# The third layer merged into the second one's block and worked batch by batch, in a kernel of four transformer layers

## What is computed

```python
# L2 xattn: a fixed mask of crucial places, maxima and means over the channels, a convolution, two maps
crucial_features = crucial_channels * x
subcrucial_features = subcrucial_channels * x
c_max = jnp.max(crucial_features, axis=1, keepdims=True)
c_avg = jnp.mean(crucial_features, axis=1, keepdims=True) * (C / k)
...
A_S1 = _norm_active(_conv1d(crucial_x, conv_w), bn_gamma, bn_beta)
A_S2 = _norm_active(_conv1d(subcrucial_x, conv_w), bn_gamma, bn_beta)
return crucial_features * A_S1 + subcrucial_features * A_S2
```

## Time and profile before

| | us |
|---|---|
| median of 3 runs | 1889.36 |
| the runs, lowest and highest | 1887.64, 1889.57 |
| the profiled execution | 1889.23 |
| its span in the trace | 1887.5 |
| TensorE (matmul) busy | 1808.7, 96% |
| DVE busy | 1348.4, 71% |
| ScalarE busy | 636.3, 34% |
| GpSimd busy | 614.9, 33% |

### The profile page before, as it was taken

How to read it: one execution, slowest core, us unless ns; L and a number is a source line. 1 busy time by engine, 2 the same in 40 slices (tenths; PEclk the granted TensorE clock), 3 DMA queues, 4 the chain that set the end, 5 groups by cost and what they waited for, 6 DMA issues and landing times. The chain is left out here.

```text
span 1887.5 us, 29022 instructions
## 1 busy us (share of the span) xinstructions
PE 1808.7 (96%) x10418; PEld 1529.3 (81%) x10418; DVE 1348.4 (71%) x2778; ACT 636.3 (34%) x1749; POOL 614.9 (33%) x366
## 2 busy tenths in 40 slices
PE   7999999999999999998998998879889999999998
PEld 6888889888988888886876664675878888888886
DVE  5666676666666676656547867788778888888886
ACT  3312222222212222224025655530343343334333
POOL 6423332233223322233141003434434333333331
PEclk9999999999999999999999998989999999999999
DMA  5101111111101111110010002010101100111111
GB/s 172 59 7 50 50 52 49 51 49 51 40 9 51 49 51 49 52 57 19 23 45 20 1 26 67 23 62 1 45 23 45 34 33 25 41 33 33 34 34 46
DMA packets 29879, 78.44 MB, mean 42 GB/s; under 512 B 3856, under 2 KB 10704, under 8 KB 29424
## 3 DMA queue, kind: packets, MB, share of 16 engines
q1 hardware_dynamic: 29808, 77.50, 12.3%
HBM read 75.39 MB, written 2.10 MB: 41 GB/s over the span
## 5 line engine op out<-in xcount | busy, mean ns | idle before, releaser
L637 POOL TENSOR_TENSOR l0x_comb<-l0x_neg,l0x_bias 128x1024 f32<-128x1024 f32 x32 | 76.5, 2391 | 428.0 <-DVE l0x_probs L1002 305.2
L900 ACT ACTIVATE l0x_probs_t<-bank 128x512 f32<-128x512 f32 x32 | 19.1, 597 | 541.5 <-PE bank L753 541.5
L2794 POOL TENSOR_TENSOR l3x_q<-l3x_q,l3x_cross 128x512 f32<-128x512 f32 x64 | 89.7, 1407 | 200.1 <-DVE l3x_q L1764 200.1
L38 PE MATMUL bank<-l0x_w_v_hi,ctx_lo 128*128 128x256 f32 x512 | 144.9, 283 | 0.0
L36 PE MATMUL bank<-l0x_w_v_hi,ctx_hi 128*128 128x256 f32 x512 | 144.9, 283 | 0.0
L37 PE MATMUL bank<-l0x_w_v_lo,ctx_hi 128*128 128x256 f32 x512 | 144.9, 283 | 0.0
L886 ACT ACTIVATE l0x_probs<-l0x_probs,l0x_top 128x129 f32<-128x129 f32 x256 | 99.4, 390 | 61.1 <-DVE l0x_top L1006 61.1
L2976 ACT ACTIVATE l3x_probs<-l3x_probs,l3x_top 128x128 f32<-128x128 f32 x256 | 99.1, 389 | 37.4 <-DVE l3x_top L3055 37.3
L629 POOL TENSOR_TENSOR l0x_w_qk_lo<-l0x_raw_qk,l0x_w_qk_hi 128x1024 fp32r<-128x1024 f32 x31 | 75.0, 2420 | 110.6 <-ACT l0x_w_qk_hi L893 110.6
L36 PE MATMUL bank<-l3x_qin_hi,l3x_w_q_hi 128*128 128x512 f32 x256 | 106.0, 414 | 3.1 <-PEq L121 3.1
L36 PE MATMUL bank<-ctx_hi,l0x_w_qk_hi 128*128 128x512 f32 x256 | 100.7, 393 | 8.5 <-DVE ctx_lo L1113 8.5
(11 more groups left out here) (474 smaller groups left out, 5233.7 us busy)
## 6 DMA issues: line engine op xcount, KB each, us to landing
l0x_raw_qk<-L_qk_dram SPq DMA_DIRECT2D x31, 512.0 KB, 5.2
l0x_raw_v<-L_v_dram SPq DMA_DIRECT2D x16, 512.0 KB, 5.6
l0x_raw_o<-L_o_dram SPq DMA_DIRECT2D x16, 512.0 KB, 5.5
l3x_raw<-L_q_dram SPq DMA_DIRECT2D x16, 512.0 KB, 3.5
l3x_raw<-L_o_dram SPq DMA_DIRECT2D x16, 512.0 KB, 3.5
kv_raw<-L_kv_dram SPq DMA_DIRECT2D x8, 512.0 KB, 3.5
l0x_ctx_raw<-ctx_t_dram SPq DMA_DIRECT2D x4, 512.0 KB, 6.4
x<-x_dram SPq DMA_DIRECT2D x8, 256.0 KB, 8.3
```

Source lines behind the costliest of these rows:

```text
L38: return pe.matmul(out, lhs[1], rhs[0], start=False, stop=stop)
L637: pool.tensor_tensor(comb[:, :, :], neg[:, :, :], bias[:, j:j + 1, :].to_broadcast([P, B, P]), ALU.add).then_inc(comb_ready, 1)
L900: act.activation(probs_t[:, 0:BH, :], bank[6][:, :].rearrange("p (b n) -> p b n", b=BH), ACT.Copy).then_inc(t_act, 1)
L2794: pool.tensor_tensor(dst[:, part], dst[:, part], cross[n][:, :], ALU.add).then_inc(rotated, 1)
```

## The change

`l1_layer` becomes `l1_and_l2`: the third layer (class `L2Layer`) is written into the second layer's block, behind its FFN on every engine, and works batch by batch. Both norms are `Handover`s. The layout of `fc` is by batch, [P, B, DC, P]; `fo` lies in the place of the normalised x; `fc` is later overwritten with the transposed input of the FFN. `take_crucial` of batch b follows the statistics of batch b + 3 (`LAG`). ScalarE makes all sums of the crucial part and those of the others for five batches (`SUMS = 5`), and these passes write to `spare` in SBUF, not into a bank; DVE makes those of three. In the last step ScalarE scales all four chunks of a batch (`scale_crucial`), DVE adds the others, scaled, in one operation for each chunk (`combine`), and GpSimd does nothing. `look_up` has three banks in place of four. The clearing of the semaphores between the two layers is gone; the one in front of the fourth layer comes at once behind the merged block. The small loads, the FFN's weights and the pieces 7 to 11 are issued behind the second layer's last `look_up`. The units: 3 between the first norm's transposes, 5 ahead of the statistics' transposes, 3, 1 and 1 in the convolution's chain, 13 behind the logits, 8 at the end.

```diff
-    ROUTE_BANKS, ATTN_BANKS, TURN_BANKS, AUX_BANKS = (5, 7), (2, 4), (2, 0), (4, 5, 3, 2)
+    ROUTE_BANKS, ATTN_BANKS, TURN_BANKS, AUX_BANKS = (5, 7), (2, 4), (2, 0), (4, 5, 3)
...
         for b in range(half * BH, (half + 1) * BH):
-            wait(pe, self.aux_read, b - 3)
-            product(pe, self.core.bank[self.AUX_BANKS[b % 4]][:, :], [self.attn_t[:, b * P:(b + 1) * P]],
+            if b == B - 1:
+                mixer.turn(pe, 0)
+            wait(pe, self.aux_read, b - 2)
+            product(pe, self.core.bank[self.AUX_BANKS[b % 3]][:, :], [self.attn_t[:, b * P:(b + 1) * P]],
                     [self.table[:, :]], True, True).then_inc(self.aux_full, 1)
...
             dve.wait_ge(self.aux_read, b + 1)
+            mixer.norm.spread(dve, b)
+            if b >= mixer.LAG:
+                mixer.take_crucial(dve, b - mixer.LAG)
...
+    def gpsimd(self, pool):
+        for b in range(B):
+            self.norm.root(pool, b)
+            if b >= BH:
+                others(b - BH)
+        for b in range(BH, B):
+            others(b)
+        ahead.low(pool, 6)
...
+    def tensor(self, pe):
+        for b in range(1, B):
+            self.turn(pe, b)
+            if b in (2, 4, 5):
+                ahead.multiply(pe, 1)
+        ahead.multiply(pe, 5)
+        pe.wait_ge(self.stat_done, 1)
+        pe.wait_ge(self.means_done, B + self.SUMS)
...
+        ahead.multiply(pe, 3)
+        pe.wait_ge(self.z_done, 1)
...
+        for b in range(B):
+            self.back(pe, b)
+            if b >= 3:
+                self.turn_again(pe, b - 3)
+            if b >= 4:
+                self.logits(pe, b - 4)
+        for b in range(B - 3, B):
+            self.turn_again(pe, b)
+            self.logits(pe, b - 1)
+        self.logits(pe, B - 1)
+        ahead.multiply(pe, 13)
...
+        ahead.multiply(pe, 8)
...
+    def sums(self, act, k, b):
+        act.wait_ge((self.fc_done, self.fo_done)[k], b + 1)
+        wait(act, self.means_done, k * B + b - 1)
+        for c in range(DC):
+            last = act.activation(self.spare[:, b % 2, c, :], (self.fo(b) if k else self.fc[:, b, :, :])[:, c, :], ACT.Copy,
+                                  scale=1.0 / (CRUCIAL, OTHERS)[k], accum_out=self.stat[:, c, 2 + k, b:b + 1])
+        last.then_inc(self.means_done, 1)
+
+    def scale_crucial(self, act, b):
+        for c in range(DC):
+            last = act.activation(self.fc[:, b, c, :], self.fc[:, b, c, :], ACT.Copy, scale=self.amap[:, c, 0, b:b + 1])
+        last.then_inc(self.scaled, 1)
...
+    def combine(self, dve, b):
+        dve.wait_ge(self.scaled, b + 1)
+        for c in range(DC):
+            last = dve.scalar_tensor_tensor(self.fc[:, b, c, :], self.fo(b)[:, c, :], self.amap[:, c, 1, b:b + 1],
+                                            self.fc[:, b, c, :], ALU.mult, ALU.add)
+        last.then_inc(self.out_ready, 1)
...
             l0_layer(core, dram)
             core.free_semaphores()
             ffn.hold_semaphores()
-            l1_layer(core, dram, ahead, ffn)
+            mixer.hold_semaphores()
+            l1_and_l2(core, dram, ahead, ffn, mixer)
         core.free_semaphores()
         with ExitStack() as kept:
             with ExitStack() as ctx_ahead:
                 ahead.hold(kept, ctx_ahead, "_place")
-                l2_attention(core, dram, ahead)
-                ahead.hold_cross(ctx_ahead)
-                l2_ffn(core, dram, ahead)
             l3_layer(core, dram, ahead, out)
```

More of the change, by code:

```diff
@@ L1215, with l1_and_l2 @@
 L1_GROUPS, L1_QUERIES, L1_DIM = 8, 4, 16
-def l1_layer(core, dram, ahead, ffn):
+def l1_and_l2(core, dram, ahead, ffn, mixer):
     nc, x, bank, psum = core.nc, core.x, core.bank, core.psum
@@ L1252, in l1_layer @@
         ffn.norm.claim()
+        mixer.norm.claim()
+        mixer.norm2.claim()
         made, same_ready, select_ready = sem("made"), sem("same_ready"), sem("select_ready")
@@ L1284, in _ @@
                 sp.wait_ge(pv_full, 2 * B - 2)
-                for i in range(8):
+                for i in range(7):
                     ahead.load(sp, i)
+                mixer.sync(sp)
             @block.gpsimd
@@ L1321, in _ @@
                 ffn.gpsimd(pool)
+                mixer.gpsimd(pool)
             @block.tensor
@@ L1467, in _ @@
                 project_out(B - 1, 1)
-                ffn.tensor(pe, o_done, B)
+                ffn.tensor(pe, o_done, B, mixer)
+                mixer.tensor(pe)
             @block.scalar
@@ L1538, in _ @@
                 ffn.scalar(act)
+                mixer.scalar(act)
             @block.vector
@@ L1624, in _ @@
                 add_out(B - 1)
-                ffn.vector(dve)
+                ffn.vector(dve, mixer)
+                mixer.vector(dve)
 KV_GROUPS = 8
@@ L1902, in turn_weights, with look_up, tensor @@
         mm.then_inc(self.t_full, 1)
-    def look_up(self, pe, half):
+    def look_up(self, pe, half, mixer=None):
         pe.wait_ge(self.t_done, half + 1)
         for b in range(half * BH, (half + 1) * BH):
-            wait(pe, self.aux_read, b - 3)
-            product(pe, self.core.bank[self.AUX_BANKS[b % 4]][:, :], [self.attn_t[:, b * P:(b + 1) * P]],
+            if b == B - 1:
+                mixer.turn(pe, 0)
+            wait(pe, self.aux_read, b - 2)
+            product(pe, self.core.bank[self.AUX_BANKS[b % 3]][:, :], [self.attn_t[:, b * P:(b + 1) * P]],
                     [self.table[:, :]], True, True).then_inc(self.aux_full, 1)
-    def tensor(self, pe, added, last):
+    def tensor(self, pe, added, last, mixer):
         self.reduce_query(pe, 0)
@@ L1935, in tensor @@
         self.turn_weights(pe, 1)
-        self.look_up(pe, 1)
-        self.ahead.multiply(pe, 2)
+        self.look_up(pe, 1, mixer)
     def copy_query(self, act, half):
@@ L2018, in scalar @@
         ahead.high(act, 5)
-        ahead.drain(act, 2)
     def copy_first(self, dve, b):
@@ L3145, in build @@
             ffn = L1Ffn(core, dram, later, ahead)
+        with ExitStack() as later:
+            mixer = L2Layer(core, dram, later, ahead, ffn)
         with ExitStack() as early:
```

748 lines of the change are left out of this document (368 added, 380 removed).

## The result

The changed kernel takes 1894.54 us (median of 6 runs, 1891.86 to 1897.52) against 1889.16 for the kernel before in the same comparison (6 runs, 1887.64 to 1889.67): a ratio of 1.003 with a 95% interval from 1.0018 to 1.0041. It is slower by 5.4 us. The forecast of 1891.8 was 2.7 us too low, and the time lies inside its range. By the prediction's own bounds (slower above 1893.1) this is the slower case, to which it gave 0.36, and not the case within, to which it gave 0.46. The profiled execution is the shortest of the six, 1891.86, with a span of 1890.1 us.

What follows compares the result with a forecast made beforehand. TensorE was taken as the bound: logits at 1259.3 plus 69.9 us end at 1329.2, +1.3; the boundary adds 1.2, so +2.5 on 1889.23, and 0.13 for the median gives 1891.8 us, range 1884.5 to 1898.5.

Steps and rivals of the forecast that it cites:

- the case within: Whole kernel: a time between the bounds for faster (below 1885.6 us) and slower (above 1893.1), chance 0.46.
- What bounds it: Whole kernel: TensorE, busy for 96% of the span; only its gaps, 24.6 us in the rewritten stretch, can be won.
- Stage A: Up to the transposes of the statistics: ScalarE ends last, transposes at 1213.2 us, 1.8 us won.
- nobody pays: Before the statistics: DVE's standing in take_crucial(0), about 6 us, costs nothing because ScalarE ends last.
- cheap sums: Rival, ScalarE's sums before the statistics: a pass stays at 0.29 us, list 4.8 us shorter, total 1887.2, chance 0.14.
- first units behind a gap: TensorE before the statistics: its clock falls while it waits, so units after that gap cost 1.3 us more.
- Stage B: The convolution's chain, statistics' transposes to map: 17.3 us plus 1.5 for units, map at 1232.0, 0.4 us won so far.
- Stage C: The last step, map to logits: DVE and ScalarE at 2.4 us per batch, 27.3 us, logits end 1259.3.
- small-piece rival: DVE's combine in the last step: each piece costs the whole 0.28 us, 2.2 us later, total 1894.0, chance 0.11.
- low-clock rival: Last step: TensorE stays at 1.2 GHz from the fourth batch on, logits 8 us later, total 1898.3, chance 0.22.
- The boundary: In front of the fourth layer: freeing the semaphores there delays the start by 1.2 us.
- D: Behind the logits: TensorE doesn't wait, units, products and FFN batches sum to 69.9 us, end at 1329.2.

Runs made afterwards that it cites:

- r3: Changed kernel with the low half of piece 5 on GpSimd behind the root of batch 5, its high half on ScalarE later: 1891.94 us, ratio 1.0015.
- r6: Changed kernel with ScalarE making the sums of the others for two batches and DVE for six: 1890.06 us, ratio 1.0002.
- r8: Changed kernel with the edits of r3, r6 and r7 together: 1883.73 us, ratio 0.9973.
- r5: The kernel before, unedited, profiled a second time: 1888.37 us (1 run).
- r12: r11 with a third unit inside the last step, behind the back of batch 3, and one ScalarE drain moved: 1884.81 us, ratio 0.9975.
- r9: Changed kernel with GpSimd scaling the fourth chunk of each batch in the last step, ScalarE three: 1894.77 us, ratio 1.0032.
- r4: The kernel before with one more clearing of semaphores in front of the fourth layer: 1891.31 us, ratio 1.0018.
- r7: Changed kernel with two of the 13 units behind the logits moved into the last step, behind backs 1 and 2: 1888.57 us, ratio 1.0.
- r11: r8 with the low half of piece 9 on GpSimd between the bias sums of batches 4 and 5: 1881.0 us, ratio 0.9958.

## Why the prediction was nearly right, point by point

**What bounds it.** Right, and it is the lesson of the case: TensorE behind the logits. r3, r6 and r8 take 2.5, 3.5 and 6.5 us from the statistics and the whole falls by 2.4, 3.4 and, with the 3.1 behind the logits, 9.7. Eleven units moved behind the logits ate the 15 us that were won in front of them: 19.7 us of units came in, 4.7 us of waits and low clock went. The sum for that stage was 69.9 us, counted from where the next unit begins; measured so it is 70.1 (1257.4 to 1327.5).

**Stage A.** The mechanism was right in the main: ScalarE ends last, and the late start of its list is on the path (r3). One step of it was wrong: "nobody pays" for DVE's six us of standing. The size was off at three terms. A pass of the sums costs 0.29 us, the end of the range that I had not taken, and not 0.385: the exp was the wrong neighbour, a copy with an accumulator into SBUF costs what it did into a bank. That is 4.8 us less, the condition of the rival "cheap sums", whose 1887.2 us didn't come for all that. ScalarE's waits on the round trips were 6.5 us and not 4.5. The longest is for TensorE's transposes of the second batch; TensorE's and then ScalarE's timeline:

```profile
1173.29 1.09 PE L247 MATMUL bank<-ident,l1f_xn 128*128 128x128 f32 x4 [4.05 <-ACT l1f_xn L240]
1176.48 2.08 PE L35 MATMUL bank<-l1f_table,l1f_attn_t 128*128 128x512 f32 x2 [2.11 <-DVE x L2122]
1178.35 1.91 PE L247 MATMUL bank<-ident,l1f_xn 128*128 128x128 f32 x8
```

```profile
1179.44 0.60 ACT L2351 ACTIVATE l1f_xn<-bank 128x512 f32<-128x512 f32 x1 [3.56 <-PE bank L247]
```

Ahead of these transposes stands `look_up`'s product of the last batch. Since there are three banks in place of four, it needs the bank that DVE's sum at 1175.7 frees, and that sum stands behind take_crucial(0), in which DVE waited its 6.08 us. So DVE's standing reaches ScalarE's list by way of TensorE. In r3 these waits are 2.07 us for TensorE and 2.34 for ScalarE. What a fourth bank, or the transposes of the first batch behind that product, would be worth no run tested.

And the 1.3 us added for first units behind a gap didn't arise ahead of the transposes, which start 0.2 us behind ScalarE's last pass. The statistics came at 1209.3 in place of 1213.2. The stage won 3.3 to 3.5 us against r5, 5.2 against the first profile.

**Stage B.** I added 1.5 us for units at a lower clock; it was 2.7. The granted clock was 0.78 in the whole stage, behind a wait of 4.4 us, and three key units stood in front of z, which started 2.7 us behind the end of DVE's taps; DVE waited 3.77 us for it. r6, which takes that wait away, brings the stage down to 18.8, r12 to 17.5, about what it was before.

**Stage C.** 27.3 us forecast, 28.1 measured up to the next unit's start (28.3 to the logits' end). A piece of combine costs 0.257 from start to start (four in 1.03), between my 0.21 and the small-piece rival's 0.28; the page VectorE: DVE Perf Modes of the Trainium skill (The TRN2 errata) gives a formula for an fp32 tensor_tensor, from which 0.29 is the estimate for such a tile. It lies above the pace of this three-operand piece when the pieces follow each other. That the measured 1894.54 lies 0.5 us from that rival's 1894.0 is chance: its piece of 0.28 didn't come. The low-clock rival didn't come in that strength: at 1238 to 1243 us, where the granted clock was 0.52, backs, turns and logits ran at the lower level (a back 1.11 us in place of 0.66), but over the stage it was 0.88. What ScalarE and GpSimd do in this step matters little (r9).

**The boundary.** The failed step: 1.2 us. From TensorE's last unit to its first matmul of the queries it is 3.1 us more than before (1327.9 to 1341.3, 1327.5 to 1344.0); the clearing alone costs 2.3 up to L141 and 2.5 in the medians (r4). I had counted the wait and not the lower clock behind it, though I had counted just that in stages A to C.

**The base of the sum.** The other failed step, and it isn't in the text at all: the sum was made against one profiled execution, as if its stretch were typical. It was 4.2 us slower from DVE's first gated sum on than r5, with lower clock at the three places shown under r5, and reached its usual total by an early start (1163.1 us in place of 1166.4).

**Luck.** Against the profile on which it was made the sum is right almost to the tenth, +2.5 forecast and +2.6 measured, and that is luck: stage A was 3.9 us too dear, and stages B, C and D and the boundary were 1.2, 0.8, 0.2 and 1.9 too cheap. Against r5 the same measured moments give +7.1 to +7.4, and the medians say +5.4 and +7.8.

**What stays open.** Executions differ by up to 8 us in the first two layers, whose code the change leaves nearly alone. The changed kernel's medians in the two comparisons differ by 2 us, and its stretch doesn't vary, so part of that 2 and of its distance to before may be such luck ahead of it. No run here separates the two layers from the rest, but nothing points at a loss of the change ahead of its stretch, for instance by the three banks of `look_up` in place of four: DVE's first gated sum starts at 1165.3 us on average in the 11 profiles with the change and at 1165.2 in the 3 without. That r3 and r6 fell by more in the medians (4.7 and, against before in each comparison, 5.6 us) than in the stretch may be the same thing. Why a clock comes back late in one execution and not in another is open; the runs show only that it does.

## What to carry to other kernels

When the work that fills one engine's gaps is moved, add up what lies behind the last point of waiting before and after: here 11 units went behind it, so 15 us of earlier logits only paid for them. What was won beyond that came from two units put back inside the gaps (r7) and from cutting the list in front at its longest engine (r3, r6). A shorter list on DVE is no gain where ScalarE's list sets the meeting point; balance the two against their measured ends, 1203.8 and 1209.1 here. And take two profiles of the kernel before and compare them stretch by stretch before a few us are argued about: one alone was 4 us off in the very place.

## What the runs showed of the hardware

After the same wait TensorE's clock can be high or low in two executions of one program (5.37 and 3.67 us for eight matmuls behind 2.55 us of waiting; 0.72, 0.86 and 1.00 granted at 962 to 974 us, in code that is the same). A little more idle at a boundary cost more by the clock than by itself: 0.85 us of wait, 1.3 us behind it (r4), though in r11 a wait of 2.46 us cost nothing behind it. ScalarE's copy of 128x128 from SBUF to SBUF with an accumulator comes every 0.29 us, as one without (0.296) and as one into a bank; the exp with an accumulator comes every 0.385. DVE's three-operand piece of 128x128 in SBUF lasts 0.34 us on average by its record and comes every 0.257.
